# One picked step per loop pass, in single buffers, and the last product of a layer returned by halves

## The chip, the cores and the metric

The kernel runs on one core of one Trainium2 chip. Its metric is the device time in microseconds (us) of one execution. The engines are called as in the profile: PE is TensorE (PEld its weight loads), DVE is VectorE, ACT is ScalarE, POOL is GpSimd, SP is SyncE; a name with a q behind it is an engine's sequencer, which takes waits, register loads and DMA issues in order.

## The reference

The input x is [32 sequences, 64 rows, 1024]. Four layers follow each other, each added to x. Only the two in the middle matter here; each multiplies every sequence by a weight picked by the sequence's id:

```
x = x + L0(x)                    # long convolution, masked by length
w = L1_weight[ids1]              # ids1: 32 numbers of 0..15, weight [16, 1024, 1024] float32
x = x + einsum('bsi,boi->bso', x, w)
w = L2_weight[ids2]              # ids2: 32 numbers of 1..14
x = x + einsum('bij,bkj->bik', x, w)
x = x + L3(x)                    # gated feed-forward with picked low-rank parts
```

The ids are drawn with a fixed seed. In the first picked layer the ids 0 to 15 come up 1, 1, 2, 2, 0, 1, 0, 4, 6, 1, 4, 1, 4, 2, 2 and 1 times; in the second 0, 0, 1, 3, 4, 2, 3, 2, 1, 5, 2, 4, 1, 2, 2 and 0 times.

## The kernel before, in words

**Steps.** All of x stays in SBUF as X, [128 partitions, 32 + 3 sequences, 8 blocks, 64 rows]; the three last places are spares. A picked layer runs over steps. A step takes one weight and up to two of the sequences that picked it; DVE works out on the chip, before the layer, which weight and which two places each step uses (`table`), and a step with one sequence takes a spare place as its second. How many loop passes a layer has is worked out there too (`turns`): the highest step number is s, and turns = round(0.5 s + 0.75), so the steps are taken in pairs and an odd number of them is filled up with one that works on spares. `STEPS` = 24 is the most there can be.

**One step.** A product of float32 precision is made of three products of a narrower kind: high part by high part, high by low, low by high. So a step needs:

- SP (line 391): the weight in four chunks of 1 MB into W[0..3], each as soon as DVE has cut the chunk of the step before (`w_lo`). There is one W for each chunk.
- ACT: the high part of each chunk (`cut_chunk`, line 727, wh from W), the high part of the two sequences' rows (`step_rows_hi`, line 741, rh from X), and the finished product out of PSUM (`copy_product`, line 732, prod from ps).
- DVE: the low parts (line 1276, wl; line 1289, rl), and the turned product added to X (`add_step`, line 1299).
- PE: `chunk` (lines 1717 to 1719), 12 matmuls of 512 columns for each of the four chunks, and `turn_product` (line 1727), eight transposes that bring the product of the step before back into X's layout.

On PE a step g is chunk 0, the transposes of step g-1, then chunks 1, 2 and 3. Chunks 0 and 1 add into one PSUM bank, which is done after chunk 1; chunks 2 and 3 into the next. Between the steps everything is handed over by counting semaphores; there is no scheduler, each engine's order is written out in its block.

**Turns of two.** rh, rl and prod have two places each and the products use four PSUM banks, one set for the even and one for the odd step. So each engine's loop body holds two steps (`picked_turn` on ACT and PE; `for half in range(2)` on SP and DVE), and the first turn is written out ahead of the loop.

**Between the layers.** The second picked layer needs the first one's X. After the last step's chunk 3, ACT copies the last bank, PE makes all eight transposes, DVE adds both sequences, ACT and DVE cut the first rows of the next layer, and only then chunk 0 follows. After the second layer `rows_done` lets the feed-forward part begin, whose first operand ACT cuts out of X (line 779).

Of the kernel before, what the change touches and what calls it, by code (L numbers as in the profile page):

```python
# [22 lines left out]
P = 128  # L23
# [15 lines left out]
WC = 4  # L39
# [9 lines left out]
assert STEPS % 2 == 0 and STEPS <= B  # L49
# [65 lines left out]
def build(nc, ins, out):  # L115
    with ExitStack() as ctx:
# [24 lines left out]
        turns = sb(early, "turns", [2, 1], I32)  # L141
# [43 lines left out]
        with ExitStack() as s:  # L185
            ident = sb(s, "ident", [P, P])
# [93 lines left out]
        turned = sem("turned")  # L280
        step_added = sem("step_added")
# [55 lines left out]
        def _(sp):  # L337
# [44 lines left out]
            for layer, w in enumerate((ins["w1"], ins["w2"])):  # L382
                count = sp.value_load(turns[layer:layer + 1, 0:1], min_val=B // 4, max_val=STEPS // 2)
                with sp.Fori(0, count) as it:
                    for half in range(2):
                        pick = sp.value_load(table[layer:layer + 1, 0, bass.ds(it * 2 + half, 1)],
                                             min_val=0, max_val=NPICK - 1)
                        for c in range(WC):

                            sp.wait_ge(w_lo, (it * 2 + (before + half)) * WC + (c + 1))  # L390
                            sp.dma_start(W[:, c], w[bass.ds(pick, 1), c].rearrange("a p i o -> (a p) i o")
                                         ).then_inc(w_in[c], 16)
                before = before + count * 2
# [298 lines left out]
        def _(act):  # L692
# [36 lines left out]
            def copy_product(g, half, o):  # L729

                act.wait_ge(chunk_done, g * WC + (2 * o + 2 + WC))
                nc.scalar.activation(prod[:, half, o * WN:(o + 1) * WN], bank(2 * half + o),
                                     ACT.Copy).then_inc(prod_copied, 1)

            def step_rows_hi(s, half, added):

                seqs = [act.value_load(table[layer:layer + 1, 1 + k, bass.ds(s, 1)],
                                       min_val=0, max_val=B + SPARE - 1) for k in range(2)]
                act.wait_ge(step_added, added)
                for k, seq in enumerate(seqs):  # L740
                    nc.scalar.activation(rh[:, half, :, k * H:(k + 1) * H],
                                         X[:, bass.ds(seq, 1)].rearrange("p a l h -> p (a l) h"),
                                         ACT.Copy).then_inc(rows_hi, 1)

            def picked_turn(it, base, first):

                for half in range(2):
# [15 lines left out]
            for layer in range(2):  # L763
                count = act.value_load(turns[layer:layer + 1, 0:1], min_val=B // 4, max_val=STEPS // 2)
                step_rows_hi(0, 0, base + 2)
                if layer == 0:
                    cut_chunk(0, 0)
# [4 lines left out]
                copy_product(base - 1, 1, 0)  # L772
                if layer == 0:
                    cut_chunk(base, 0)
                copy_product(base - 1, 1, 1)
# [256 lines left out]
        def _(dve):  # L1032
# [185 lines left out]
            def count_turns():  # L1218
# [41 lines left out]
            stages = [number_steps, count_turns, find_members, place_members]  # L1260
# [8 lines left out]
            V.memset(tick[:, 2:3], 0.0).then_inc(chunk_done, WC)  # L1269
            V.memset(tick[:, 3:4], 0.0).then_inc(step_added, 2)  # L1270
# [8 lines left out]
            def place(s, k):  # L1279
                return dve.value_load(table[layer:layer + 1, 1 + k, bass.ds(s, 1)],  # L1280
                                      min_val=0, max_val=B + SPARE - 1)

            def step_rows_lo(s, g, half):

                for k in range(2):
                    seq = place(s, k)
# [721 lines left out]
```

## Time and profile before

| | us |
|---|---|
| three runs | 2271.15, 2274.89, 2275.08; median 2274.89 |
| the profiled execution | 2274.16 |
| its span, first to last instruction | 2272.5 |
| PE busy | 2126.8 (94% of the span) |
| DVE busy | 1626.6 (72%) |
| ACT busy | 978.2 (43%) |
| picked layers, first to last matmul | from 208.4 to 694.3 of the span |
| weight chunks cut | 160 on ACT and 160 on DVE |

The span runs from the first to the last instruction; 1.7 us of the execution lie around it. A busy share is an average over all stages. In the views below, a group's row gives the engine, the operation, out<-in, its count, then busy time and mean; "idle ... <-" behind it is how long the engine stood still ahead of it and what ended that. "issue" means that nothing the profile records ended the wait.

### The profile page before, as it was taken

What the parts mean: (1) busy time and instruction counts of PE and PEld (TensorE: products, weight loads), DVE (VectorE), ACT (ScalarE), POOL (GpSimd) and SP (SyncE); (2) the same over time, 40 slices, a digit from 0 to 9 for tenths busy, and PEclk for the clock granted to TensorE, in tenths of its full rate; (3) what the DMA queues carried; (4) which work ended last, traced back from release to release, by engine and by line L of the source; (5) the groups of instructions that cost most, each with busy time, mean ns of one, the idle gap of its engine ahead of it and who ended that gap; (6) DMA issues with size and microseconds to landing.
All of it is one profiled execution on the core that took longest, in us unless ns stands there. A gap on an engine that the chain in (4) does not pass through costs nothing.

```text
span 2272.5 us, 33796 instructions
## 1 busy us (share of the span) xinstructions
PE 2126.8 (94%) x10544; PEld 1800.9 (79%) x10544; DVE 1626.6 (72%) x2079; ACT 978.2 (43%) x1222; POOL 99.4 (4%) x167
## 2 busy tenths in 40 slices
PE   2998999999996999999998399999999999999998
PEld 2997888788885788888887288888888888878886
DVE  7777999899996878878785135648878888743433
ACT  2213778778774443434332024334333433322232
POOL 3211000000001330000000000000000000000000
PEclk9999999999998999999999699999999999999999
DMA  5999999989995664334335945443434333354543
GB/s 196 388 364 341 349 350 344 343 319 356 352 350 226 194 197 117 101 95 113 93 95 180 212 151 184 168 148 100 108 97 108 92 104 103 84 192 152 182 142 129
DMA packets 255810, 449.87 MB, mean 198 GB/s; under 512 B 147030, under 2 KB 147222, under 8 KB 234518
## 3 DMA queue, kind: packets, MB, share of 16 engines
q1 hardware_dynamic: 242198, 417.08, 55.4%
q0 software_dynamic: 11392, 32.01, 4.3%
q10 hardware_dynamic: 2176, 0.26, 0.1%
q8 instruction: 19, 0.31, 0.1%
q14 instruction: 25, 0.20, 0.0%
HBM read 409.13 MB, written 63.73 MB: 208 GB/s over the span
## 4 chain that ended last, share of the span: by engine, by line
PE 83%; DVE 7%; DMA 3%; SPq 2%; issue 2%; ACT 2%; DVEq 0%; POOL 0%; ACTq 0%; POOLq 0%
PE ps L1756 18%; PE ps L1757 18%; PE ps L1758 18%; PE ps L1717 6%; PE ps L1719 6%; PE ps L1718 6%; PE ps L1694 3%; SPq L522 2%; PE ps L1800 2%; PE ps L1801 2%; PE ps L1727 2%; DMA wraw<-in_wd 1%; DMA araw<-picked_a 1%; PE ps L1832 1%; PE ps L1833 1%
## 5 line engine op out<-in xcount | busy, mean ns | idle before, releaser
L1756 PE MATMUL ps<-bh,oph 128*128 128x512 f32 x1216 | 478.2, 393 | 9.6 <-ACT tmp L779 6.0
L1757 PE MATMUL ps<-bl,oph 128*128 128x512 f32 x1216 | 477.9, 393 | 0.0
L1758 PE MATMUL ps<-bh,opl 128*128 128x512 f32 x1216 | 476.2, 392 | 0.0
L1276 DVE TENSOR_TENSOR wl<-W,wh 128x2048 fp32r<-128x2048 f32 x160 | 362.8, 2287 | 29.8 <-ACT wh L727 29.3
L1337 DVE TENSOR_TENSOR wdl<-wraw,wdh 128x1024 fp32r<-128x1024 f32 x92 | 112.7, 1225 | 326.1 <-ACT wdh L779 326.0
L1340 DVE TENSOR_TENSOR tmp<-ps,tmp 128x512 f32<-128x512 f32 (+1 forms) x340 | 234.1, 689 | 136.7 <-PE ps L1801 75.0
L1756 PE MATMUL ps<-acb_h,wdh 128*128 128x512 f32 (+1 forms) x736 | 282.4, 384 | 47.2 <-DVE acb_l L1337 43.0
L727 ACT ACTIVATE wh<-W 128x2048 fp32r<-128x2048 f32 x160 | 302.1, 1911 | 37.9 <-DMA W<-in_w 32.7
L1757 PE MATMUL ps<-acb_l,wdh 128*128 128x512 f32 (+1 forms) x736 | 281.5, 382 | 0.0
L1758 PE MATMUL ps<-acb_h,wdl 128*128 128x512 f32 (+1 forms) x736 | 281.3, 382 | 0.0
L1756 PEld LDWEIGHTS ps<-bh,oph 128*128 128x128 f32 x1216 | 230.7, 190 | 55.5 <-DVE opl L1337 10.8
L1758 PEld LDWEIGHTS ps<-bh,opl 128*128 128x128 f32 x1216 | 230.2, 189 | 49.1
L1717 PE MATMUL ps<-wh,rh 128*128 128x512 f32 x640 | 257.2, 402 | 12.1 <-DVE wl L1276 7.6
L1757 PEld LDWEIGHTS ps<-bl,oph 128*128 128x128 f32 x1216 | 230.6, 190 | 43.4
L779 ACT ACTIVATE wdh<-wraw 128x1024 fp32r<-128x1024 f32 x92 | 97.5, 1059 | 378.4 <-PE ps L1758 307.3
L1719 PE MATMUL ps<-wh,rl 128*128 128x512 f32 x640 | 251.5, 393 | 0.0
L1718 PE MATMUL ps<-wl,rh 128*128 128x512 f32 x640 | 251.1, 392 | 0.0
L779 ACT ACTIVATE oph<-sraw 128x512 fp32r<-128x512 f32 x168 | 106.1, 632 | 281.2 <-PE ps L1758 153.9
L1756 PEld LDWEIGHTS ps<-acb_h,wdh 128*128 128x128 f32 x736 | 139.6, 190 | 76.0 <-DVE wdl L1337 41.0
L1758 PEld LDWEIGHTS ps<-acb_h,wdl 128*128 128x128 f32 x736 | 139.5, 190 | 26.9
L1757 PEld LDWEIGHTS ps<-acb_l,wdh 128*128 128x128 f32 x736 | 139.7, 190 | 26.3
L1717 PEld LDWEIGHTS ps<-wh,rh 128*128 128x128 f32 x640 | 121.3, 190 | 43.9 <-issue 20.0
(204 smaller groups left out, 2840.9 us busy)
## 6 DMA issues: line engine op xcount, KB each, us to landing
W<-in_w SPq DMA_DIRECT2D x160, 1024.0 KB, 6.2
raw<-in_wgu SPq DMA_DIRECT2D x168, 256.0 KB, 2.7
wraw<-in_wd SPq DMA_DIRECT2D x84, 512.0 KB
toep<-kpad SPq DMA_DIRECT2D x32, 1024.0 KB, 9.2
lraw<-picked_b SPq DMA_DIRECT2D x88, 256.0 KB, 4.0
raw<-kept_acts SPq DMA_DIRECT2D x88, 256.0 KB, 3.4
kept_acts<-tmp SPq DMA_DIRECT2D x84, 256.0 KB, 2.2
picked_b<-in_lora_b POOLq DMA_DIRECT2D x32, 352.0 KB, 4.6
```

The costliest lines, as they stand in the source:

```text
L727: nc.scalar.activation(wh[:, c], W[:, c], ACT.Copy).then_inc(w_hi, 1)
L779: return nc.scalar.activation(to, src, ACT.Copy)
L1276: V.tensor_tensor(out=wl[:, c], in0=W[:, c], in1=wh[:, c].bitcast(F32), op=ALU.subtract).then_inc(w_lo, 1)
L1337: return V.tensor_tensor(out=to, in0=a, in1=b, op=ALU.subtract)
L1340: return V.tensor_tensor(out=to, in0=a, in1=b, op=ALU.add)
L1694: last = mm(ps[:, i % RING, (e + 1) * LT * B - n:(e + 1) * LT * B], lhsT=toep[:, i % RING, e, d * P:(d + 1) * P], rhs=rows[:, 0:n], start= ...
L1717: mm(to, lhsT=rh[:, half, at], rhs=wh[:, c, k], start=first, stop=False)
L1718: mm(to, lhsT=rh[:, half, at], rhs=wl[:, c, k], start=False, stop=False)
L1719: last = mm(to, lhsT=rl[:, half, at], rhs=wh[:, c, k], start=False, stop=end)
L1756: mm(to, lhsT=wh, rhs=mh, start=start, stop=False)
L1757: mm(to, lhsT=wh, rhs=ml, start=False, stop=False)
L1758: return mm(to, lhsT=wl, rhs=mh, start=False, stop=stop)
```

## The change

The picked layers' loops take one step per pass. rh and rl have one place, written by halves: the half of the rows that chunks 0 and 1 use, and the half that chunks 2 and 3 use. prod has one place and the products two banks. For this the host lays the weight's chunks out in another order: chunks 0 and 1 are now the first half of the input rows for output halves 0 and 1, chunks 2 and 3 the second half of the input rows. So bank 0 is done after chunk 2 and bank 1 after chunk 3. The number of passes is the number of steps (`counts`), with no filling up. The last step of a layer is written out on PE: after three quarters of chunk 3 it transposes output half 0, and half 1 at the end; DVE adds the two halves apart, and on ACT and DVE the next layer's first step is woven between them.

What moves on ACT, the loop body of one step. Before (the first of the two steps in a body; rh is the rows' high part, wh a chunk's, prod the product out of PSUM):

```order
L727 ACTIVATE wh<-W 128x2048 [waits chunk_done]
...
L741 ACTIVATE rh<-X 128x8x64
L741 ISA
L741 ACTIVATE rh<-X 128x8x64
L731 ISA
L732 ACTIVATE prod<-ps 128x512 [waits chunk_done]
L726 REGISTER_ALU [waits w_in1]
L727 ACTIVATE wh<-W 128x2048 [waits chunk_done]
L731 REGISTER_ALU
L732 ACTIVATE prod<-ps 128x512 [waits chunk_done]
L726 REGISTER_ALU [waits w_in2]
```

And now:

```order
L745 ACTIVATE rh<-X 128x4x64
L728 ACTIVATE wh<-W 128x2048 [waits chunk_done,w_in1]
L732 ISA
L734 ACTIVATE prod<-ps 128x512 [waits turned,chunk_done]
L727 REGISTER_ALU [waits w_in2]
L728 ACTIVATE wh<-W 128x2048 [waits chunk_done]
L732 REGISTER_ALU
L734 ACTIVATE prod<-ps 128x512 [waits turned,chunk_done]
L742 REGISTER_ALU
L745 ISA [waits chunk_done]
L745 ACTIVATE rh<-X 128x4x64
```

The rows' high part is cut in four instructions of 256 elements, where there were two of 512, two of them behind the second copy of the product; chunk 2's cut stands ahead of that copy.

On PE, the end of a layer. Before (ident is the transposes' operand, turns the loop count of the next layer):

```order
L1727 MATMUL ps<-ident,prod 128x128 [waits step_added]
L1727 MATMUL ps<-ident,prod 128x128 x7
L1746 TENSOR_LOAD turns
L1746 ISA x2
L1734 ISA
L1712 ISA [waits rows_cut]
L1717 MATMUL ps<-wh,rh 128x512 [waits w_lo]
```

And now, from the last quarter of the last chunk on:

```order
L1767 MATMUL ps<-ident,prod 128x128 [waits step_added]
L1767 MATMUL ps<-ident,prod 128x128 x3
L1758 MATMUL ps<-wh,rh 128x512
L1759 MATMUL ps<-wl,rh 128x512
L1760 MATMUL ps<-wh,rl 128x512
L1797 REGISTER_ALU
L1767 MATMUL ps<-ident,prod 128x128 [waits prod_copied]
L1767 MATMUL ps<-ident,prod 128x128 x3
L1804 TENSOR_LOAD counts
```

Four of the eight transposes stand ahead of the chunk's last three matmuls.

The diff, cut to its core:

```diff
-            rh = sb(s, "rh", [P, 2, LT, 2 * H], F32R)
-            rl = sb(s, "rl", [P, 2, LT, 2 * H], F32R)
-            prod = sb(s, "prod", [2 * H, 2, L])
+            rh = sb(s, "rh", [P, LT, 2 * H], F32R)
+            rl = sb(s, "rl", [P, LT, 2 * H], F32R)
+            prod = sb(s, "prod", [2 * H, L])
...
# ACT
-            def picked_turn(it, base, first):
-
-                for half in range(2):
-                    s = it * 2 + half
-                    g = base + s
-                    lag = not (first and half == 0)
-                    if lag:
-                        cut_chunk(g, 0)
-                        step_rows_hi(s, half, g + 1)
-                        copy_product(g - 1, 1 - half, 0)
-                    cut_chunk(g, 1)
-                    if lag:
-                        copy_product(g - 1, 1 - half, 1)
-                    cut_chunk(g, 2)
-                    cut_chunk(g, 3)
+            def picked_step(it, g):
+
+                cut_chunk(g, 0)
+                seqs = places(it)
+                act.wait_ge(step_added, g + 1)
+                step_rows_hi(seqs, g, 0)
+                cut_chunk(g, 1)
+                copy_product(g - 1, 0)
+                cut_chunk(g, 2)
+                copy_product(g - 1, 1)
+                step_rows_hi(seqs, g, 1)
+                cut_chunk(g, 3)
...
+                    cut_chunk(base, 0)
+                    cut_chunk(base, 1)
+                    copy_product(base - 1, 0)
+                    act.wait_ge(half_added, 1)
+                    step_rows_hi(seqs, base, 0)
+                    copy_product(base - 1, 1)
+                    cut_chunk(base, 2)
+                    act.wait_ge(step_added, base + 2)
+                step_rows_hi(seqs, base, 1)
...
# DVE
-                link(V.tensor_scalar(found[:, 0, 0:1], found[:, 0, 0:1], 0.5, 0.75, ALU.mult, ALU.add))
-                round_turns(found[:, 0, 0:1])
-                link(V.tensor_copy(turns[:], found[:, 0, 0:1]))
+                link(V.tensor_scalar_add(found[:, 0, 0:1], found[:, 0, 0:1], 1.0))
+                link(V.tensor_copy(counts[:], found[:, 0, 0:1]))
...
+            def picked_step(it, g):
+
+                cut_chunk(g, 0)
+                both = places(it, layer)
+                step_rows_lo(both, g, 0)
+                cut_chunk(g, 1)
+                cut_chunk(g, 2)
+                step_rows_lo(both, g, 1)
+                add_step(it - 1, g - 1)
+                cut_chunk(g, 3)
...
                 if layer == 0:
                     cut_chunk(base, 0)
-                add_step(count * 2 - 1, base - 1)
+                    cut_chunk(base, 1)
+                add_last_half(last, 0, base - 1)
+                if layer == 0:
+                    both = places(0, 1)
+                    step_rows_lo(both, base, 0)
+                    add_last_half(last, 1, base - 1)
+                    cut_chunk(base, 2)
+                    step_rows_lo(both, base, 1)
+                    cut_chunk(base, 3)
+                else:
+                    add_last_half(last, 1, base - 1)
...
# PE
+            def picked_step(g, first=False, last=False):
+
+                pe.wait_ge(rows_cut, g * 4 + 4)
                 pe.wait_ge(prod_copied, g * 2 + 2)
+                chunk(g, 0)
+                if not first:
+                    turn_product(g - 1)
+                pe.wait_ge(prod_copied, g * 2 + 3)
+                chunk(g, 1)
+                pe.wait_ge(rows_cut, g * 4 + 6)
+                chunk(g, 2)
+                if not last:
+                    chunk(g, 3)
+                    return
+                chunk(g, 3, range(WK - 1))
+                pe.wait_ge(prod_copied, g * 2 + 4)
                 pe.wait_ge(step_added, g + 2)
+                turn_half(0).then_inc(half_turned, 1)
+                chunk(g, 3, range(WK - 1, WK))
+                pe.wait_ge(prod_copied, g * 2 + 5)
+                turn_half(1).then_inc(turned, 1)
...
-                picked_turn(0, base, True)
-                with pe.Fori(1, count) as it:
-                    picked_turn(it, base, False)
-                base = base + count * 2
-                turn_product(base - 1, 1)
+                picked_step(base, first=True)
+                with pe.Fori(1, count - 1) as it:
+                    picked_step(base + it)
+                base = base + count
+                picked_step(base - 1, last=True)
```

## Rows read from the trace of the kernel before

**Rows 1.** Busy time per stretch: PE, PEld, DVE, ACT, POOL, clock, DMA.

```profile
420.00:460.00 40.00, 34.96 (x155) 28.25 (x154) 33.46 (x25) 27.63 (x25) 0.00 (x0) 0.91 0.80 299
540.00:580.00 40.00, 40.00 (x193) 33.11 (x192) 37.58 (x27) 32.69 (x28) 0.00 (x0) 1.00 0.93 354
```

**Rows 2.** Page, costliest groups: DVE's cuts of weight chunks.

```profile
L1276 DVE TENSOR_TENSOR wl<-W,wh 128x2048 fp32r<-128x2048 f32 x160 | 362.8, 2287 | 29.8 <-ACT wh L727 29.3
```

**Rows 3.** Chain of waits, transposes of three steps: start, length, what.

```profile
613.79 0.87 PE ps L1727 x8
...
625.61 0.87 PE ps L1727 x8
...
637.59 0.87 PE ps L1727 x8
```

**Rows 4.** Page, DMA queues for instructions: packets, MB, share.

```profile
q8 instruction: 19, 0.31, 0.1%
q14 instruction: 25, 0.20, 0.0%
```

**Rows 5.** DVE in time order, one step.

```profile
613.34 2.29 DVE L1276 TENSOR_TENSOR wl<-W,wh 128x2048 fp32r<-128x2048 f32 x1 [0.50 <-ACT wh L727]
...
616.75 4.49 DVE L1276 TENSOR_TENSOR wl<-W,wh 128x2048 fp32r<-128x2048 f32 x2
621.15 1.28 DVE L1289 TENSOR_TENSOR rl<-X,rh 128x512 fp32r<-128x512 f32 x2
622.35 2.28 DVE L1276 TENSOR_TENSOR wl<-W,wh 128x2048 fp32r<-128x2048 f32 x1
625.34 2.29 DVE L1276 TENSOR_TENSOR wl<-W,wh 128x2048 fp32r<-128x2048 f32 x1 [0.71 <-ACT wh L727]
```

**Rows 6.** Weight chunks' DMAs, issue to landing, whole program.

```profile
DMA to landing us min/median/max: 4.7/6.2/11.6
```

**Rows 7.** Groups by form: a DVE subtraction of 256 elements.

```profile
L1337 DVE TENSOR_TENSOR adt<-adraw,adt 128x256 fp32r<-128x256 f32 x44 | 18.7, 426 | 1.3
```

**Rows 8.** In time order, from the first layer's end on: ACT, DVE, PE.

```profile
448.15 0.39 PE L1719 MATMUL ps<-wh,rl 128*128 128x512 f32 x1
448.58 0.60 ACT L732 ACTIVATE prod<-ps 128x512 f32<-128x512 f32 x1 [3.04 <-PE ps L1719]
...
449.31 1.09 PE L1727 MATMUL ps<-ident,prod 128*128 128x128 f32 x8 [0.77 <-ACT prod L732]
450.54 0.69 DVE L1299 TENSOR_TENSOR X<-ps,X 128x512 f32 x1 [2.67 <-PE ps L1727]
451.39 0.69 DVE L1299 TENSOR_TENSOR X<-ps,X 128x512 f32 x1 [0.16 <-issue]
452.22 1.15 ACT L741 ACTIVATE rh<-X 128x512 fp32r x2 [3.05 <-DVE X L1299]
...
454.67 0.79 PE L1717 MATMUL ps<-wh,rh 128*128 128x512 f32 x1 [4.27 <-DVE rl L1289]
...
459.46 0.40 PE L1719 MATMUL ps<-wh,rl 128*128 128x512 f32 x1
```

**Rows 9.** PE in time order, two other idle times and the clock behind them.

```profile
1219.24 0.39 PE L1800 MATMUL ps<-tmh,lt 128*128 128x256 f32 x1 [2.19 <-DVE tmp L1340]
...
1220.91 0.63 PE L1757 MATMUL ps<-bl,oph 128*128 128x512 f32 x1
```

```profile
1391.28 0.47 PE L1756 MATMUL ps<-acb_h,wdh 128*128 128x512 f32 x1 [1.01 <-DVE resid L1340]
```

**Rows 10.** In time order, the end of the second layer.

```profile
693.88 0.39 PE L1719 MATMUL ps<-wh,rl 128*128 128x512 f32 x1
...
697.12 0.69 DVE L1299 TENSOR_TENSOR X<-ps,X 128x512 f32 x1 [0.17 <-issue]
```

**Rows 11.** PE in time order, its one idle time inside a layer.

```profile
353.01 0.49 PE L1717 MATMUL ps<-wh,rh 128*128 128x512 f32 x1 [0.25 <-DVE rl L1289]
```

**Rows 12.** PE idle for nothing recorded, behind another loop.

```profile
191.48 9.36 PE L1694 MATMUL ps<-urev,toep 128*128 128x256 f32 x64 [0.65 <-issue]
```

More of the change, by code:

```diff
@@ L48 @@
 SPARE = 3
-assert STEPS % 2 == 0 and STEPS <= B
+assert STEPS <= B
 FF = 2752
@@ L727, in cut_chunk, with copy_product @@
                 nc.scalar.activation(wh[:, c], W[:, c], ACT.Copy).then_inc(w_hi, 1)
[L729 to L737, printed above, removed]
+            def copy_product(g, o):
+                act.wait_ge(chunk_done, g * WC + (o + 3 + WC))
+                act.wait_ge(turned, g + 1)
+                nc.scalar.activation(prod[:, o * WN:(o + 1) * WN], bank(o), ACT.Copy).then_inc(prod_copied, 1)
@@ L1277, in cut_chunk @@
                                 op=ALU.subtract).then_inc(w_lo, 1)
[L1279 to L1286, printed above, removed]
-                    dve.wait_ge(rows_hi, g * 2 + (k + 1))
-                    mine = slice(k * H, (k + 1) * H)
-                    V.tensor_tensor(out=rl[:, half, :, mine],
-                                    in0=X[:, bass.ds(seq, 1)].rearrange("p a l h -> p (a l) h"),
-                                    in1=rh[:, half, :, mine].bitcast(F32), op=ALU.subtract).then_inc(rows_cut, 1)
@@ new lines, in turned_rows @@
+            def turned_rows(seq, k, at, n):
+                rows = X[:, bass.ds(seq, 1), at * WK:(at + n) * WK].rearrange("p a l h -> p (a l) h")
+                return V.tensor_tensor(out=rows, in0=ps[:, TURN + at:TURN + at + n].rearrange(
+                    "p c (l w) -> p (c l) w", w=2 * H)[:, :, k * H:(k + 1) * H], in1=rows, op=ALU.add)
+            def add_step(s, g):
+                for k, seq in enumerate(places(s, layer)):
+                    dve.wait_ge(turned, g + 2)
+                    ins_ = turned_rows(seq, k, 0, 2)
+                ins_.then_inc(step_added, 1)
@@ new lines, in add_last_half, with places @@
+            def add_last_half(both, at, g):
+                if at == 0:
+                    dve.wait_ge(half_turned, layer + 1)
+                else:
+                    dve.wait_ge(turned, g + 2)
+                for k, seq in enumerate(both):
+                    ins_ = turned_rows(seq, k, at, 1)
+                ins_.then_inc(half_added if at == 0 else step_added, 1)
+            def places(s, at):
+                return [dve.value_load(table[at:at + 1, 1 + k, bass.ds(s, 1)],
+                                       min_val=0, max_val=B + SPARE - 1) for k in range(2)]
@@ L1707, in _ @@
                     convolve(c, i)
-            def chunk(g, half, c):
-                pe.wait_ge(w_lo, g * WC + (c + 1 + WC))
-                to = bank(2 * half + c // 2)
-                for k in range(WK):
-                    at = (c % 2) * WK + k
-                    first, end = at == 0, at == LT - 1
-                    mm(to, lhsT=rh[:, half, at], rhs=wh[:, c, k], start=first, stop=False)
-                    mm(to, lhsT=rh[:, half, at], rhs=wl[:, c, k], start=False, stop=False)
-                    last = mm(to, lhsT=rl[:, half, at], rhs=wh[:, c, k], start=False, stop=end)
-                last.then_inc(chunk_done, 1)
@@ L1722, in turn_product, with chunk @@
-            def turn_product(g, half):
-                pe.wait_ge(prod_copied, g * 2 + 2)
-                pe.wait_ge(step_added, g + 2)
-                for o in range(LT):
-                    last = nc.tensor.transpose(ps[:, TURN + o // 4, (o % 4) * P:(o % 4 + 1) * P],
-                                               prod[:, half, o * P:(o + 1) * P], ident[:])
-                last.then_inc(turned, 1)
-            def picked_turn(it, base, first):
-                for half in range(2):
-                    g = base + it * 2 + half
-                    pe.wait_ge(rows_cut, g * 2 + 2)
-                    chunk(g, half, 0)
-                    if not (first and half == 0):
-                        turn_product(g - 1, 1 - half)
-                    chunk(g, half, 1)
-                    chunk(g, half, 2)
-                    chunk(g, half, 3)
+            def chunk(g, c, blocks=range(WK)):
+                half, o = c // 2, c % 2
+                if blocks[0] == 0:
+                    pe.wait_ge(w_lo, g * WC + (c + 1 + WC))
+                for k in blocks:
+                    at = half * WK + k
+                    first, end = at == 0, at == LT - 1
+                    mm(bank(o), lhsT=rh[:, at], rhs=wh[:, c, k], start=first, stop=False)
+                    mm(bank(o), lhsT=rh[:, at], rhs=wl[:, c, k], start=False, stop=False)
+                    last = mm(bank(o), lhsT=rl[:, at], rhs=wh[:, c, k], start=False, stop=end)
+                if blocks[-1] == WK - 1:
+                    last.then_inc(chunk_done, 1)
```

122 lines of the change are left out of this document (67 added, 55 removed).

## The prediction

> **What bounds the kernel now.** I read the page first: PE is busy 94% of the span, so what counts is what PE does and where it stands. Then the busy time by stretches, to see the picked layers alone: from 540 to 580 us PE is busy 40.00 of 40 us at full clock, DVE 37.6, ACT 32.7, and the DMA engines 93% of the time; around the change of layers, 420 to 460, PE has only 34.96 at a granted clock of 0.91 [rows 1]. So inside a layer PE bounds and DVE and the weight's transfers are close behind; between the layers it is a chain through ACT and DVE. Third the chain of waits for the pace of a step, and last the rows in time order around the two ends of layers.
>
> Steps: the groups count 160 chunk cuts [rows 2], four a step, which is 40 steps, 20 a layer. The ids give the number needed: for each id half its count, rounded up. First layer 1+1+1+1+0+1+0+2+3+1+2+1+2+1+1+1 = 19, second 0+0+1+2+2+1+2+1+1+3+1+2+1+1+1+0 = 19. Both are odd, so each layer now runs one filling step, with all its matmuls, cuts and 4 MB of weight.
>
> **The pace of a step.** Transposes start at 613.79, 625.61 and 637.59 [rows 3]. The distances are 11.82 and 11.98, and so they alternate all along the layer: every second one holds the loop's branch. A step takes 11.82 and a branch about 0.16 more.
>
> **Two steps less.** 2 x 11.82 = -23.6. That is PE time at 100% busy; nothing covers it, and the DMA, ACT and DVE parts of the step go with it. PE can't gain more inside a step, as it has no idle time there.
>
> **More branches.** Before, the loop's nine passes a layer each began behind a branch (18 in all). Now there are 17 passes and the fall out of the loop into the written-out last step, 18 a layer. 18 more in two layers x 0.16 = +2.9. Bounds: nothing if the branch hides behind queued matmuls, and 0.65 each from the only idle time of PE behind a loop that nothing recorded ended [rows 12], +11.7. I take 0.16, since it is the row of the same loop.
>
> A rule speaks against this term: the Trainium skill, Runtime: NRT & Kernel Launch, section Instruction fetch mechanics, says that a taken branch whose target lies outside the instruction window forces a fetch before the engine goes on. The trace doesn't show that here: the two queues for instructions moved 44 packets in the whole execution [rows 4], and the branches of the picked loop alone are 18 a sequencer. By that rule the term would grow towards the rival of fetches below.
>
> **Inside a step, will PE still run without a stop?** Let PE's chunk 0 start at 0: chunk 0 to 2.7, transposes to 3.65, chunks 1, 2, 3 end at 6.4, 9.1 and 11.8 (12 matmuls of 0.227 each; that pace is read between rows 3). DVE's work in a step is 12.00 less 0.71 idle, 11.3 [rows 5]. Its pieces overlap: the pair of 512 takes 1.20 from start to next start, the cuts 2.20. Now the rows' low part comes in four pieces of 256; one alone takes 0.43 [rows 7], and with the overlap seen (0.69 alone, 0.60 in a row) about 0.345. So 4 x 0.345 - 1.20 = +0.18, and DVE's step is 11.5 against PE's 11.98. It fits, with 0.5 left. ACT gets a like amount more and has more room, 32.7 of 40 [rows 1].
>
> The single buffers set these dates. ACT can copy bank 1 at 0.25 (chunk 3 of the step before has just ended) to 0.85, then cut the second half of rows to 1.6; DVE cuts their low part behind chunk 2, at 3.4; PE needs them at 6.4. Bank 0 is copied at about 9.3 to 9.9 and PE writes it again at 12.0. The transposes need bank 1's copy at 2.7. DVE adds at 3.75 (behind the transposes, a wait of some 0.4 that takes the place of its wait for ACT), cuts chunk 3 to 7.2, and with chunk 0 at 9.4, half rows, chunks 1 and 2 comes to its next add at 15.2, before the transposes end at 15.65. What queues behind that add on DVE is chunk 3's cut, done at 7.2 and wanted by PE at 9.1. The weight's ring: W[0] is free at 9.4, lands 6.2 later [rows 6] at 15.6, is cut on ACT to 17.5, and DVE wants it at 19.2. W[1] is free at 12.3, lands at 18.5; ACT gets to it at 19.2. Slack 0.7 to 1.7. So I put stalls inside the step at 0. Bounds: 0, and 0.35 a step if every step were as the worst one before: in one place of a layer the slack ran out, and PE stood for 0.25 until the low rows were cut [rows 11].
>
> **Between the layers.** I count from the start of the last chunk 3. Before: its last matmul starts at 2.50 (448.15 in the trace), the next layer's first at 454.67, 6.52 later, so at 9.02 [rows 8]. Now: nine matmuls to 2.04, four transposes to 2.49, the rest to 3.4. First half: the add starts 1.23 behind eight transposes' start [rows 8], with four fewer 0.79, so at 2.83; two adds of 256, 0.77; ACT 0.14 later, at 3.74. From there to PE's start it was 2.45 (452.22 to 454.67); of the pieces in a row three are now of 256, each 0.26 shorter (0.69 less 0.43 [rows 7]), so 1.7: the rows are there at 5.4. Second half: ACT copies bank 1 only behind those cuts of rows, at 4.4; transposes 0.73 later as before, at 5.15; four of them and the loop count's load, then chunk 0 at about 5.75. So bank 1's way is the later one, and the gain is 9.02 - 5.75 = -3.2. Its second half of rows comes at about 10, needed at 11.2. Bounds: 0 if ACT is still at chunk 1's cut for the next layer when bank 0 is ready, and -3.9 if the second half hides wholly.
>
> **The clock there.** Behind the long idle time the first 11 matmuls start 0.43 apart, to 459.46 [rows 8]: the lower of the two levels, 1.2 GHz; 4.79 for what takes 2.5, a loss of 2.3. Now PE stands from 3.4 to 5.15, 1.8 us. In the trace an idle time of 2.19 was followed by matmuls 0.43 apart for 8 of them, 1.7 lost, one of 1.01 by none [rows 9]. 1.8 is nearer to 2.19, so I take a fall again and 1.7 lost: -0.6. Other end: no fall, -2.3.
>
> On this the Trainium skill, TensorE: Matmul & The Clock Gate, section Why this matters for your kernels, asks for no idle gap over about 3 us; by it 1.8 us would leave the clock alone and the sum would be 1.7 lower. The row with 2.19 disagrees, and the measurement decides.
>
> **The end of the second layer.** Same halves without the rows: before, the last matmul starts at 2.50 and the last add ends 3.93 later (693.88 to 697.81 [rows 10]), at 6.43; now copy at 3.4, transposes 4.1, adds 4.9 to 5.65: -0.8. All that follows hangs on this add and shifts with it. Bounds 0 and -1.2.
>
> **The start.** Rows cut in halves let chunk 0's cut begin 0.4 earlier on ACT; three more tiny memsets stand ahead, +0.1: -0.3, bounds 0 and -0.4.
>
> **Sum.** -23.6 + 2.9 - 3.2 - 0.6 - 0.8 - 0.3 = -25.6. Against the profiled execution, 2274.16, that is 2248.6. The runs' median is 0.7 above that execution, so 2249 for a median of runs.
>
> **The rivals.**
> Ring stalls (0.15): the weight's transfers, 93% busy, land late often enough that PE waits 0.3 a step; 36 steps, +11: 2260. For it: rows 11, and the slack of 0.7 above. Against: 40.00 of 40.
> Fetches (0.03): every one of the 36 branches costs 0.65 [rows 12]: 23.4 where 5.8 is counted, 2267. Against: the same loop's 0.16.
> No steps go (0.04): if the step numbers ran to 20 a layer, both filling steps stay: 2249 + 2 x 11.98 = 2273, no change that could be told. The trace's 40 steps fit 19 and 20 alike; against it stands only the count of ids.
> DVE bounds (0.04): short pieces stop overlapping, since register loads and waits stand between them, as behind the layer's end, where two adds stood 0.16 apart [rows 8]. Then a step on DVE is 4 x 2.45 + 4 x 0.59 + 2 x 0.85 = 13.9, 1.9 over PE's, 36 times: +68, 2317, slower. It would be slower than before from a DVE step of about 12.8 on. Against: the pairs overlap in every step of rows 5, with the same register loads between them.
> Better (0.04): branches free and no fall of the clock: 2249 - 2.9 - 1.7, 2244.
>
> **How the numbers follow.** The forecast has 0.70, by itself 2245 to 2254. With the ring stalls and the better case, and the bounds above, 8 in 10 lie in 2242 to 2262. A change of 0.2%, 4.5 us, is about what runs can tell. Faster: 0.70 + 0.15 + 0.03 + 0.04 = 0.92; same 0.04; slower 0.04.
>
> **What would show it.** 152 chunk cuts on DVE and ACT, not 160; transposes 11.98 apart in every step, with PE busy all of a stretch of 40 us; DVE's rl in 152 pieces of about 0.43, and its idle time moved from ACT's wh to PE's transposes; PE idle for about 1.8 us between the layers and chunk 0 some 3 us sooner; matmuls 0.43 apart behind it or not. Wrong if PE shows idle times inside the loop ended by wl, rl or prod, if the distance of transposes passes 12.2, or if 160 cuts remain.

## The result

| | before | changed |
|---|---|---|
| median of 4 runs each, us | 2273.74 | 2240.36 |
| lowest and highest | 2271.15, 2275.08 | 2238.03, 2240.67 |
| profiled execution | 2274.16 | 2240.67 |
| its span | 2272.5 | 2239.0 |

The ratio is 0.9854 (95%: 0.9842 to 0.9867): 33 us faster, where the prediction had 25.6 and a range that ended 1.6 us above the result. The direction and the largest term were right; a second gain was not seen coming.

The page of the changed kernel, the group that answers to [rows 2] and the two instruction queues of [rows 4]:

```profile
L1292 DVE TENSOR_TENSOR wl<-W,wh 128x2048 fp32r<-128x2048 f32 x152 | 343.2, 2286 | 7.1 <-ACT wh L728 6.3
```

```profile
q8 instruction: 18, 0.29, 0.1%
q14 instruction: 23, 0.19, 0.0%
```

152 cuts are 38 steps, 19 a layer, as counted from the ids. With twice as many loop passes, the queues for instructions moved 41 packets, where they had moved 44. DVE's idle time for ACT's cuts, 29.3 in all before, is 6.3. The stretches of [rows 1]:

```profile
420.00:460.00 40.00, 37.95 (x179) 31.13 (x178) 37.16 (x36) 32.54 (x33) 0.00 (x0) 1.00 0.89 338
540.00:580.00 40.00, 39.80 (x188) 32.85 (x187) 38.76 (x34) 34.38 (x36) 0.00 (x0) 1.00 0.95 351
```

The change of layers now stands earlier in the first one, so it has more PE time, and no low clock in this execution. In the second, where [rows 1] read 40.00, PE reads 39.80. The missing 0.20 is one idle time, the only one inside the layers:

```profile
564.59 1.92 ACT L728 ACTIVATE wh<-W 128x2048 fp32r<-128x2048 f32 x1 [0.69 <-DMA W<-in_w]
566.41 0.58 ACT L734 ACTIVATE prod<-ps 128x512 f32<-128x512 f32 x1
...
567.13 0.49 PE L1758 MATMUL ps<-wh,rh 128*128 128x512 f32 x1 [0.20 <-ACT prod L734]
```

ACT waited 0.69 for a weight chunk, so the copy behind its cut came late, and PE waited for the copy; the two transposes around it are 12.26 apart. For the rest the busy share can't tell whether a step got shorter. The distance of the transposes can. The chain of waits, as [rows 3]:

```profile
593.72 0.87 PE ps L1767 x8
605.52 0.87 PE ps L1767 x8
617.30 0.87 PE ps L1767 x8
```

11.80 and 11.78: each step has a loop branch, and each takes what before only the shorter of two took. The layers' change, all engines in time order (start, length, engine, line, operation; idle time before in brackets), as [rows 8]:

```profile
433.85 0.60 PE L1767 MATMUL ps<-ident,prod 128*128 128x128 f32 x4
...
434.75 0.40 PE L1760 MATMUL ps<-wh,rl 128*128 128x512 f32 x1
...
436.90 0.66 PE L1767 MATMUL ps<-ident,prod 128*128 128x128 f32 x4 [1.75 <-ACT prod L734]
...
437.85 0.49 PE L1758 MATMUL ps<-wh,rh 128*128 128x512 f32 x1 [0.30 <-issue]
438.19 0.40 PE L1759 MATMUL ps<-wl,rh 128*128 128x512 f32 x1
438.42 0.39 PE L1760 MATMUL ps<-wh,rl 128*128 128x512 f32 x1
```

From the last matmul to the next layer's first it is 3.10, where it was 6.52. PE stands twice, 1.75 and 0.30, and the matmuls behind start 0.23 apart at once: 2.4 GHz, no fall. It is bank 1's way that comes last, as forecast. The end of the second layer, as [rows 10]:

```profile
661.82 0.40 PE L1760 MATMUL ps<-wh,rl 128*128 128x512 f32 x1
...
663.71 0.76 DVE L1308 TENSOR_TENSOR X<-ps,X 128x256 f32 x2 [1.29 <-PE ps L1767]
```

And the start of the first:

```profile
205.66 0.76 DVE L1301 TENSOR_TENSOR rl<-X,rh 128x256 fp32r<-128x256 f32 x2 [2.31 <-issue]
...
208.77 0.76 PE L1758 MATMUL ps<-wh,rh 128*128 128x512 f32 x1 [7.51 <-DVE wl L1292]
```

**Where 33.5 us of span went** (the terms are rounded). Before, the first layer ran 239.75 from its first to its last matmul start (208.40 to 448.15), the second 239.21; now 225.98 (208.77 to 434.75) and 223.97 (437.85 to 661.82). The transposes' distances say the same: in the first layer 17 of them take 202.8 before and 200.4 now. The four transposes that now stand inside chunk 3 (0.36, 433.85 to 434.21) are put to the ends of layers below.

| term | predicted | the two traces |
|---|---|---|
| two steps less, at 11.82 | -23.6 | -23.6 |
| pace of the other 38 steps, branches in it | +2.9 | -3.8 |
| between the layers | -3.2 | -3.1 (6.52 to 3.10 + 0.36) |
| clock behind it | -0.6 | -2.3 |
| end of the second layer | -0.8 | -0.9 (3.93 to 2.65 + 0.36) |
| start | -0.3 | -0.1 |
| convolution before, which ended later by itself | | +0.4 |
| behind the picked layers | | -0.2 |
| sum | -25.6 | -33.6 |

The pace's -3.8 is what is left of each layer: 225.62 - 239.75 + 11.82 = -2.3 and, without 2.3 of low clock, 223.61 - 239.21 + 11.82 + 2.3 = -1.5. The pace differs from the forecast by 6.7 of the 7.9 in question.

### The profile page after: what moved, and what is told of

Its sections match the earlier page's. It is cut to its first block, busy times and chain, and to the rows that moved or that the text cites. A ratio compares the mean times of both kernels' runs of the same rounds, so it can differ in the third digit from the quotient of the medians.

```text
span 2239.0 us, 34126 instructions
## 1 busy us (share of the span) xinstructions
PE 2097.4 (94%) x10432; PEld 1782.3 (80%) x10432; DVE 1610.1 (72%) x2144; ACT 971.7 (43%) x1282; POOL 98.6 (4%) x167
## 4 chain that ended last, share of the span: by engine, by line
PE 78%; DVE 9%; DMA 5%; issue 3%; ACT 2%; SPq 2%; DVEq 1%; POOL 0%; ACTq 0%; POOLq 0%
PE ps L1814 18%; PE ps L1815 18%; PE ps L1816 18%; PE ps L1758 4%; PE ps L1760 4%; PE ps L1759 4%; PE ps L1734 4%; DMA W<-in_w 3%; SPq L523 2%; PE ps L1858 2%; PE ps L1859 2%; DVE wl L1292 2%; PE ps L1767 1%; DMA wraw<-in_wd 1%; DMA araw<-picked_a 1%
## 5 line engine op out<-in xcount | busy, mean ns | idle before, releaser
L1292 DVE TENSOR_TENSOR wl<-W,wh 128x2048 fp32r<-128x2048 f32 x152 | 343.2, 2286 | 7.1 <-ACT wh L728 6.3
L728 ACT ACTIVATE wh<-W 128x2048 fp32r<-128x2048 f32 x152 | 290.5, 1915 | 52.5 <-DMA W<-in_w 48.0
L1758 PE MATMUL ps<-wh,rh 128*128 128x512 f32 x608 | 241.6, 397 | 8.0 <-DVE wl L1292 7.5
L1760 PE MATMUL ps<-wh,rl 128*128 128x512 f32 x608 | 238.1, 392 | 0.0
L1759 PE MATMUL ps<-wl,rh 128*128 128x512 f32 x608 | 237.6, 391 | 0.0
L1734 PE MATMUL ps<-urev,toep 128*128 128x256 f32 (+7 forms) x1024 | 150.3, 309 | 1.4 <-issue 0.8
```

The costliest lines, as they stand in the source:

```text
L728: nc.scalar.activation(wh[:, c], W[:, c], ACT.Copy).then_inc(w_hi, 1)
L1292: V.tensor_tensor(out=wl[:, c], in0=W[:, c], in1=wh[:, c].bitcast(F32), op=ALU.subtract).then_inc(w_lo, 1)
L1734: last = mm(ps[:, i % RING, (e + 1) * LT * B - n:(e + 1) * LT * B], lhsT=toep[:, i % RING, e, d * P:(d + 1) * P], rhs=rows[:, 0:n], start= ...
L1758: mm(bank(o), lhsT=rh[:, at], rhs=wh[:, c, k], start=first, stop=False)
L1759: mm(bank(o), lhsT=rh[:, at], rhs=wl[:, c, k], start=False, stop=False)
L1760: last = mm(bank(o), lhsT=rl[:, at], rhs=wh[:, c, k], start=False, stop=end)
```

## Why a step got faster

**Theory A, the branch:** PE's branch costs 0.16, as predicted, and something else hides it now. **Theory B, a chain:** before, a chain of waits PE, ACT, DVE, PE (a ring, as it ends where it began) came back later than PE by itself, and PE waited for it a little in every second step; the new order shortens it. In the expectations below, theory 1 is B and theory 2 is A.

What B rests on is in the trace of before. ACT (with its wait for PE's chunk 3), then DVE, then PE:

```profile
575.31 0.60 ACT L732 ACTIVATE prod<-ps 128x512 f32<-128x512 f32 x1 [2.53 <-PE ps L1719]
575.80 5.51 ACT L727 ACTIVATE wh<-W 128x2048 fp32r<-128x2048 f32 x3
...
587.08 0.60 ACT L732 ACTIVATE prod<-ps 128x512 f32<-128x512 f32 x1 [2.27 <-PE ps L1719]
```

```profile
577.75 2.29 DVE L1276 TENSOR_TENSOR wl<-W,wh 128x2048 fp32r<-128x2048 f32 x1 [0.73 <-ACT wh L727]
579.96 1.28 DVE L1299 TENSOR_TENSOR X<-ps,X 128x512 f32 x2
581.15 4.48 DVE L1276 TENSOR_TENSOR wl<-W,wh 128x2048 fp32r<-128x2048 f32 x2
585.56 1.29 DVE L1289 TENSOR_TENSOR rl<-X,rh 128x512 fp32r<-128x512 f32 x2
...
597.33 1.29 DVE L1289 TENSOR_TENSOR rl<-X,rh 128x512 fp32r<-128x512 f32 x2
```

```profile
586.66 0.39 PE L1719 MATMUL ps<-wh,rl 128*128 128x512 f32 x1
586.98 0.49 PE L1717 MATMUL ps<-wh,rh 128*128 128x512 f32 x1
587.30 0.40 PE L1718 MATMUL ps<-wl,rh 128*128 128x512 f32 x1
...
598.90 0.40 PE L1717 MATMUL ps<-wh,rh 128*128 128x512 f32 x1
```

Chunk 3 ends at 575.3, ACT copies the bank (0.60), only then cuts chunk 2 (to 577.7); DVE cuts its low part, adds, cuts chunks 3 and 0 and then the low rows, which are done at 586.85. PE's next chunk 0 starts at 586.98. Matmuls inside a chunk start 0.227 apart; the two distances at 586.98 are 0.32 each, 0.19 lost. None of it shows as idle time, since a matmul's modelled length, 0.39, is longer than the distance of two starts. So "40.00 of 40 busy" could not tell that PE waited. What a step takes if nothing waits is 48 x 0.227 + 0.87 = 11.77; the mean of before was 11.9.

The same rows give the alternation without a branch. The copy that starts a round waits for the last matmul of chunk 3, 586.66, which stands ahead of the late start at 586.98; so the lateness doesn't reach the copy at 587.08, but only the one after it, at 599.11. From copy to low rows both rounds take 11.54 (575.31 to 586.85, 587.08 to 598.62), though each engine's loop branch falls into only one of the two. The second comes in time for PE, which starts chunk 0 at 598.90 without a loss; the first did not. This is read from one pair of steps.

In the changed kernel chunk 2's cut stands ahead of the second copy, and chunk 0 wants only half of the rows. Run 3 below undoes the first of these; the second by itself was not tested.

### 1. Twenty steps, the new way

```diff
-                link(V.tensor_scalar_add(found[:, 0, 0:1], found[:, 0, 0:1], 1.0))
+                link(V.tensor_scalar_add(found[:, 0, 0:1], found[:, 0, 0:1], 2.0))
```

> The changed kernel with 20 steps in each picked layer in place of 19 (the count that DVE works out is one higher; the twentieth step works on spare places). Both theories of the step's pace say the same: two steps more at the changed kernel's 11.79 us, +23.6 on 2240.4, so 2264. If the 33 us had come from elsewhere (the loops' form alone), the time would stay near 2240.

Measured 2264.03 (8 runs, 2262.13 to 2267.81), 0.9971 (0.9961 to 0.9982) of the kernel before beside it (2271.74). Against the changed kernel's 2240.36, measured at another time, the two filling steps cost 23.7, 11.8 each; against run 4, measured beside this one, 23.1. The transposes stand 11.77 and 11.81 apart with a branch between each. With 20 steps a layer 7.7 us of gain are left. This run doesn't divide them: the pace, the change of layers and the end are all in them.

### 2. The kernel before, chunk 2's cut ahead of the copy

```diff
                     if lag:
+                        cut_chunk(g, 2)
                         copy_product(g - 1, 1 - half, 1)
-                    cut_chunk(g, 2)
```

(on ACT, with the cut once in either case.)

> The kernel before with one exchange on ACT: chunk 2's high part is cut ahead of the second copy of the product, not behind it. Theory 1 (a chain sets the step: end of chunk 3, ACT copies bank 2 and then cuts chunk 2, DVE cuts it, adds, cuts chunks 3 and 0 and the rows' low part, PE's next chunk 0; 11.9 a step): the chain is cut, the transposes come 11.79 apart without alternation, 40 x 0.11 = 4.4 us less, 2269.4, and PE no longer takes its chunk 0 at the end of rl. Theory 2 (each pass through the loop's branch costs 0.16): distances alternate 11.82 and 11.98 as before, 2273.7.

Measured 2269.17 (11 runs, 2266.57 to 2273.96), 0.9986 (0.9977 to 0.9995): -2.6 us, where B expected some -4.3 and A 0. The interval, -1.1 to -5.2, holds B's and not A's. The trace is clearer. Its chain of waits, in the same part of the layer:

```profile
563.53 0.87 PE ps L1727 x8
575.33 0.87 PE ps L1727 x8
587.11 0.88 PE ps L1727 x8
598.91 0.87 PE ps L1727 x8
```

11.80, 11.78, 11.80, with the loop in turns of two untouched. The 11.98 is gone though the branch is still there: A falls. Late in the second layer two distances were 12.08 and 11.97 all the same. There ACT waited 2.13 and 0.54 for weight chunks, DVE 0.48 and 0.16 for ACT's cuts, and the low rows were done at 643.18, 0.13 before PE's late start at 643.31: late weights, by this trace.

### 3. The changed kernel, chunk 2's cut last

```diff
                 copy_product(g - 1, 0)
-                cut_chunk(g, 2)
                 copy_product(g - 1, 1)
                 step_rows_hi(seqs, g, 1)
+                cut_chunk(g, 2)
                 cut_chunk(g, 3)
```

> The changed kernel with chunk 2's cut on ACT behind the second copy of the product and the second half of rows, where the copy stood ahead of it in the kernel before. Theory 1: the chain is back and longer: from chunk 3's end copy 0.5, rows 0.7, cut 1.9, DVE's cut 2.2, rows 0.7, add 1.2, cut of chunk 3 2.2 give PE's chunk 3 some 9.8 after the last one's end, and with its own 2.7 a step of 12.5; 36 steps x 0.75 = +27, 2267. Theory 2: no instruction is added and the branches are the same, so 11.79 a step and 2240.

Measured 2267.70 (10 runs), 0.9982 (0.9973 to 0.9991), B's number within 1 us: this one line, moved behind a copy and half of the rows, gives back 27 of the 33 us. By the trace the pace is 25 of them (34 distances within the layers, 0.73 longer each in the mean); the rest is at the change of layers, where PE stands for 2.90 and the clock falls. The ring can be read in the trace, ACT, DVE and PE:

```profile
602.35 0.60 ACT L734 ACTIVATE prod<-ps 128x512 f32<-128x512 f32 x1 [1.11 <-PE ps L1760]
...
603.46 1.91 ACT L728 ACTIVATE wh<-W 128x2048 fp32r<-128x2048 f32 x1
605.40 2.29 DVE L1292 TENSOR_TENSOR wl<-W,wh 128x2048 fp32r<-128x2048 f32 x1 [1.08 <-ACT wh L728]
...
607.61 0.76 DVE L1301 TENSOR_TENSOR rl<-X,rh 128x256 fp32r<-128x256 f32 x2
608.28 1.28 DVE L1308 TENSOR_TENSOR X<-ps,X 128x512 f32 x2
...
609.48 4.48 DVE L1292 TENSOR_TENSOR wl<-W,wh 128x2048 fp32r<-128x2048 f32 x2
...
611.82 0.50 PE L1758 MATMUL ps<-wh,rh 128*128 128x512 f32 x1
...
614.88 0.60 ACT L734 ACTIVATE prod<-ps 128x512 f32<-128x512 f32 x1 [0.29 <-PE ps L1760]
```

Chunk 3's end (602.3), copy, rows, cut of chunk 2, on DVE its low part, rows, add and the first of two cuts (chunk 3's, to 611.77), PE's chunk 3 at 611.82 and the next copy at 614.88: 12.53 a round, which is the distance of nearly all transposes here.

### 4. PE's loop in bodies of two steps

```diff
-                with pe.Fori(1, count - 1) as it:
-                    picked_step(base + it)
+                picked_step(base + 1)
+                with pe.Fori(0, 8) as it:
+                    picked_step(base + 2 + it * 2)
+                    picked_step(base + 3 + it * 2)
```

> The changed kernel with PE's loop body holding two steps (one step written out ahead of it, eight passes of two), all other engines as they are. Theory 1: nothing changes, 11.79 a step and 2240.4. Theory 2 in the form that a branch costs only behind a long body, as in the kernel before: distances alternate 11.79 and 11.95, 16 passes and two entries, +2.9, 2243.

Measured 2240.92 (4 runs), 0.9863 (0.9848 to 0.9878), distances 11.77 to 11.81 as before the edit, but for one of 11.97. The changed kernel had 2240.36 and 2240.72 at other times. PE's branch in every step or in every second one makes no difference that can be told, and with runs 1 and 2 it is settled that PE doesn't pay the 0.16 for it here.

## The ends of the layers

### 5. The last product whole

ACT, DVE and PE go back to one copy of both banks, eight transposes and whole adds behind the last chunk 3. PE's part:

```diff
-                chunk(g, 3, range(WK - 1))
-                pe.wait_ge(prod_copied, g * 2 + 4)
-                pe.wait_ge(step_added, g + 2)
-                turn_half(0).then_inc(half_turned, 1)
-                chunk(g, 3, range(WK - 1, WK))
-                pe.wait_ge(prod_copied, g * 2 + 5)
-                turn_half(1).then_inc(turned, 1)
+                chunk(g, 3)
+                if last:
+                    turn_product(g)
```

> The changed kernel with the last product of a layer returned whole, as in the kernel before: all eight transposes behind chunk 3, one add for each sequence, the next layer's rows behind both. If the halves are worth what the trace of the changed kernel shows: 2.3 between the layers (the old chain of 6.52 less 0.8 for the rows' shorter pieces, against 3.10, and 0.36 of transposes moved out of chunk 3), 0.9 at the end of the second layer, and 2.3 for the clock if the idle time of some 4 us lets it fall: 2240.4 + 5.5 = 2245.9. If PE's steps alone decide: 2240.4.

Measured 2244.12 (4 runs, 2241.44 to 2246.59), 0.9872 (0.9846 to 0.9898), and the changed kernel, run again beside it as number 8, 2240.72: 3.4 us for the halves. With four runs each the two intervals overlap, so the times alone make the size uncertain. Its trace at the change of layers, PE:

```profile
435.01 0.39 PE L1759 MATMUL ps<-wh,rl 128*128 128x512 f32 x1
...
440.75 0.79 PE L1757 MATMUL ps<-wh,rh 128*128 128x512 f32 x1 [3.51 <-DVE rl L1300]
441.34 0.63 PE L1758 MATMUL ps<-wl,rh 128*128 128x512 f32 x1
441.77 0.63 PE L1759 MATMUL ps<-wh,rl 128*128 128x512 f32 x1
```

5.74 from the last matmul to the first, where 3.10 stood, and behind the 3.51 of idle time matmuls 0.43 apart for 5.7 us, the lower of the two levels, 1.2 GHz. From the last transposes inside the old layer's loop to the first of the new layer it is 31.0 here, 26.1 in the changed kernel's first trace and 27.7 in its second (number 8). So gap and clock are worth 3.4 to 4.9 by the traces, where 2.3 + 2.3 was expected. At the end of the second layer it is 3.67 from the last matmul to the end of the last add, against 2.65 + 0.36: 0.7, for 0.9.

### 6. ACT copies the last bank before the new rows

```diff
                     copy_product(base - 1, 0)
+                    copy_product(base - 1, 1)
                     act.wait_ge(half_added, 1)
                     step_rows_hi(seqs, base, 0)
-                    copy_product(base - 1, 1)
```

> The changed kernel with ACT copying the last bank between the layers ahead of the first cuts of rows, not behind them. In the changed kernel's trace PE waits 1.75 for that copy, which stands behind the cuts. By that the second half's transposes start 1.0 earlier, the rows' low part becomes the later way, and chunk 0 of the next layer starts about 0.35 earlier: 2240.0. The rival: the cuts of rows were the later way already, then chunk 0 comes 0.5 later, 2240.9.

Measured 2239.99 (4 runs), 0.9853 (0.9828 to 0.9878); the changed kernel beside it 2240.72. That is no difference that these runs can tell. The trace:

```profile
435.48 0.40 PE L1760 MATMUL ps<-wh,rl 128*128 128x512 f32 x1
436.56 0.66 PE L1767 MATMUL ps<-ident,prod 128*128 128x128 f32 x4 [0.69 <-ACT prod L734]
438.52 0.49 PE L1758 MATMUL ps<-wh,rh 128*128 128x512 f32 x1 [1.31 <-DVE rl L1301]
```

The transposes come 1.1 sooner, and now the rows come last: 3.04 instead of 3.10, a gain of 0.06 where 0.35 was expected. The idle times of 1.75 and 0.30 became 0.69 and 1.31, and the clock stayed up. What that is worth the times don't show.

### 7. The first chunk of all cut in four blocks

PE's first matmuls wait for a quarter of chunk 0, not for all of it; ACT and DVE, with number 6's edit kept (DVE's half):

```diff
-                    cut_chunk(base, 0)
+                    for k in range(WK):
+                        dve.wait_ge(*((first_hi, k + 1) if k < WK - 1 else (w_hi, 1)))
+                        V.tensor_tensor(out=wl[:, 0, k], in0=W[:, 0, k], in1=wh[:, 0, k].bitcast(F32),
+                                        op=ALU.subtract).then_inc(first_lo if k < WK - 1 else w_lo, 1)
```

> The same, and the very first chunk of the first picked layer is cut in four blocks of 512 on ACT and DVE, each taken by PE as it comes. PE stands 7.5 us ahead of this layer for a chain of rows 0.8, cut 1.9 and low part 2.3; with blocks the first needs 0.6 and 0.7, so PE starts 2.8 earlier: 2237.2. At the lower clock PE takes 1.28 a block, DVE cuts one in 0.6 to 0.7, so it stays ahead. The rival: the start is bound by the second chunk's cut or by the DMA, then 2240.

Measured 2238.61 (4 runs, 2237.01 to 2239.57), 0.9849 (0.9824 to 0.9874), between the two expected numbers. PE's idle time ahead of the picked layers fell from 7.42 (number 6) to 5.83, 1.6 and not 2.8:

```profile
204.33 2.17 ACT L775 ACTIVATE wh<-W 128x512 fp32r<-128x512 f32 x4
205.79 0.76 DVE L1307 TENSOR_TENSOR rl<-X,rh 128x256 fp32r<-128x256 f32 x2 [2.23 <-issue]
...
207.30 0.76 PE L1770 MATMUL ps<-wh,rh 128*128 128x512 f32 x1 [5.83 <-DVE wl L1358]
```

ACT's four blocks begin at 204.33, when the high rows are there, but DVE starts at 205.79, behind 2.23 of idle time in which it waits for nothing: its sequencer loads the step count and two places. The same 2.31 stands in the changed kernel's start, above. It is why the halved rows gave next to nothing there (-0.1 for -0.3).

Most of the earlier start does not last. In the third step PE waits 0.39 for the low rows, as DVE had waited for ACT and ACT for weight chunks (1.34 and 0.77), and the distance of the transposes is 12.49. From the start of the convolution's last add to the layer's third transposes it is 45.13 here. It is 45.30, 45.47 and 45.49 in numbers 6, 8 and 10, which have no blocks and about as many matmuls 0.43 apart at the start (five or six). So 0.2 to 0.4 of the 1.6 is left: the rival that named the DMA is in good part right.

### 9. The same, with these loads ahead of the wait

```diff
+            dve.wait_ge(table_ready, 1)
+            count0 = dve.value_load(counts[0:1, 0:1], min_val=B // 2, max_val=STEPS)
+            both0 = places(0, 0)
```

(ahead of the small memsets that tell ACT that x is done; the same loads behind them are left out.)

> The kernel with the first chunk by blocks, and DVE's three register loads (the count and two places) put ahead of its wait for the last convolution's rows. With the blocks alone PE started only 1.6 us earlier, not 2.8, and DVE's first instruction of this layer, the rows' low part, began 2.3 behind its memsets. If the loads hold it up (0.55, 0.32 and 0.31 with their register work), rl starts at once behind ACT's rows, PE 1.5 earlier again, and the time is 2237.1, 3.6 under the changed kernel beside it. The rival: ACT's cut of the first block is what DVE waits for, and nothing changes from 2238.6.

Measured 2238.29 (5 runs, 2237.17 to 2240.69), 0.9850 (0.9836 to 0.9864), idle time 5.47: 0.4 less, where up to 1.5 was expected. Here too a distance of 12.59 follows, and the third transposes stand 45.54 behind the start of the last add. Ten matmuls at the start are 0.43 apart in this trace; the changed kernel's first trace, with eleven, has 46.59, so with the lower clock for as long some 0.8 to 1.0 is left. The loads did not run beside the convolution's last add, they ran behind its issue and held up the memsets instead:

```profile
204.58 1.03 DVE L1168 TENSOR_TENSOR X<-masked,u 128x512 f32<-128x512 f32 x1
206.87 0.06 DVE L1295 MEMSET tick<- 1x1 f32 x1 [1.26 <-issue]
```

My expectation failed. A load moved ahead of an instruction in the same order moves that instruction back.

### 8 and 10. The changed kernel again

> The changed kernel once more, beside the three others: 2240.4. Its clock between the layers is the question: with the same idle time of about 1.75 it either stays at full speed as in its first profile, or falls, as it did behind 1.59 with PE's loop in pairs; a fall costs 1.7.

> The changed kernel beside the one above, for the comparison on one chip: 2240.5.

2240.72 (4 runs, 2238.37 to 2242.43) and 2239.36 (5 runs, 2237.72 to 2242.08), beside 2273.84 and 2271.38 before: ratios 0.9854 (0.9829 to 0.9879) and 0.9851 (0.9837 to 0.9865). They also settle the clock term. Number 8 at the layers' change:

```profile
435.83 0.66 PE L1767 MATMUL ps<-ident,prod 128*128 128x128 f32 x4 [1.59 <-ACT prod L734]
...
437.86 0.63 PE L1758 MATMUL ps<-wh,rh 128*128 128x512 f32 x1
438.29 0.63 PE L1759 MATMUL ps<-wl,rh 128*128 128x512 f32 x1
```

Matmuls 0.43 apart from 437.45 on, for 3.4 us: the clock fell behind 1.59 of idle time, four transposes and another 0.39. It did so in number 10 as well (1.59) and in number 4, and it did not in the changed kernel's first trace (1.75) nor in number 1 (1.79). The fall costs 1.6: the way from the last transposes to the new layer's was 2.89 + 16.41 there and 3.05 + 14.68 without. The Trainium skill (TensorE: Matmul & The Clock Gate, section Why this matters for your kernels) asks for no idle gap over about 3 us; three traces with 1.59 disagree, and two with 1.75 and 1.79 agree. The profiled executions fit, 2242.43 and 2242.08 with the fall, 2240.67 without.

But number 8's is longer for another cause too. Between 511 and 654 us twelve distances of its transposes add up to 143.08, 1.6 more than twelve of 11.79, the longest 12.13. At one of them PE starts a chunk at 532.28, 0.13 behind the end of ACT's copy, and that copy stands behind a cut for which ACT had waited 0.40 for the weight. This is the stall in the ring that the prediction had as a rival, at a small size. Number 10's second layer has 0.2 of it.

Numbers 7 and 9 have the lowest medians, 2.1 and 1.1 us below the changed kernel beside them. Their intervals overlap with its own, and their traces show a gain of 0.2 to 1.0 at the start. So they beat the kernel before, and against the changed one they are not shown better.

## Why the prediction was right and where it failed

- **Two steps less** held: 152 cuts, 11.6 to 11.8 us a step by run 1. The rival in which no steps go is out.
- **"A step takes 11.82 and a branch about 0.16 more"** is the step that failed, with "PE can't gain more inside a step, as it has no idle time there". Only that every second distance held a branch was seen; that it was the branch's cost was inferred from a coincidence. Runs 2 and 3 show that ACT's order sets the pace: the old steps waited for a chain through ACT's copy and chunk 2's cut. Run 4 shows that PE pays nothing for its branch. The term was +2.9 and the traces have -3.8. Both of the views that misled me, busy 40.00 of 40 and no idle row, are blind below 0.16 a start (0.39 - 0.227). A sum would have shown it: 48 x 0.227 + 0.87 = 11.77, and the trace had 11.98. I made a timetable for the new step, whose dates are 0.3 to 0.8 early (in the step whose chunk 0 starts at 590.83 the adds come 4.0 later, for 3.75, and the next chunk 0's cut is done 10.2 later, for 9.4); I never made one for the old.
- **Inside a step no stall** held nearly: DVE's idle time moved from ACT's cuts (44 times, 29.3 before; 23, 6.3 now) to PE's transposes (22 times, 13.6). The rivals of fetches and of DVE's bound did not come. The ring's stalls came at a small size: one of 0.20 on PE, ended by prod (one of the forecast's own signs of being wrong), worth 0.5 with its step of 12.26, and 1.6 in number 8, where the rival had 11. The slack was put too high: weight chunks landed after 6.8 in the median, not 6.2, and ACT waited 48.0 in all for them. DVE is close to binding too, with 38.76 of 40.
- **Between the layers**: -3.1 for -3.2, and bank 1's way last, by the same chain. Run 5 gives 3.4 to 4.9 for gap and clock of the halves, for 4.6 expected of them.
- **The clock**: a fall was assumed, 1.7. In three traces of this kernel it came twice, at 1.6. The term is right for these two, and for the first the other end that was named, -2.3, is: 1.7 of the forecast's error. The choice by the length of the idle time is not borne out, as the fall came behind the shorter ones.
- **The end** -0.9 for -0.8. **The start** -0.1 for -0.3: the sequencer's loads on DVE hold it, which were not in the working.
- The rival named Better (2244: branches free, no fall of the clock) had the nearest size, with 0.04. Its branches are free and in the first trace the clock did not fall; what it lacked is that the old steps waited. The range was set by the branch's bounds on the slow side and had nothing for a gain inside a step, because PE was read as full. That bound should have been reckoned from the 11.77.

## What to carry to other kernels

To ask whether PE waits, add up: instructions times their closest spacing, against the time from one repeat to the next; a busy share of 100% made of modelled matmul ends says nothing at the level of 1%. When one of two repeats is longer, look for what each engine's last wait releases before you give it to the one difference you know, and make the timetable for the old order too. In an engine's fixed order, put what the next engine in the ring needs early ahead of what it needs late: one cut moved behind a copy and half of the rows cost 27 us here, and exchanging it with the copy alone brought 2.6 in the kernel before.

## What the runs showed of the hardware

- Loops of 56 and of 112 matmul and transpose instructions on PE, with a branch every 11.79 or 23.6 us (the changed kernel and number 4), run at the same pace, within 0.02 of the 11.77 that matmuls and transposes alone add up to; in the changed kernel the two instruction queues moved 41 packets in all. The fetch that the Trainium skill (Runtime: NRT & Kernel Launch, section Instruction fetch mechanics) puts behind a taken branch out of the window is not visible in them; whether loops of this length leave that window, no run here shows.
- No one bound of idle time divides these traces: the same kernel, at the same place, fell to 1.2 GHz behind 1.59 (numbers 8 and 10) and not behind 1.75 (its first trace). It did not fall in the three traces in which the idle time was cut in two pieces of at most 1.37 (numbers 6, 7 and 9), and it fell behind 2.90 and 3.51 (numbers 3 and 5).
- Two subtractions back to back on DVE overlap by 0.08 to 0.09 at both sizes seen in the changed kernel: one of 256 elements takes 0.42, two 0.76; of 2048 one takes 2.29, two 4.49.
- A load of a number out of SBUF into DVE's sequencer takes 0.30 or 0.31, and the arithmetic behind it 0.19 (number 3's chain of waits); the three at the start of the changed kernel's layers took 0.50, 0.40 and 0.32. It delays what stands behind it in the order (number 9).
